# Attention and gated MLP in one fp32 kernel: both rows of a step turned and moved as one, values fetched whole a head ahead, two projections placed behind weighted sums

## What is computed

```python
k, q, v = (einsum('ihd,bpd->biph', W, xn) for W in (W_K, W_Q, W_V))
scores  = einsum('biph,biqh->biqp', k, q)
masked  = scores * mask - 1e10 * (1 - mask)
attn    = softmax(masked / sqrt(128))
z       = einsum('biqp,biph->biqh', attn, v)
out     = einsum('df,bqf->bqd', W_O, z_flat)
```

## Time and profile before

| | us |
|---|---|
| median of 3 runs | 1621.35 |
| lowest and highest | 1618.32, 1623.26 |
| the profiled execution's own time | 1623.7 |
| span of its profile | 1621.7 |
| PE busy | 1414.5 |
| POOL busy | 994.6 |
| DVE busy | 955.6 |
| ACT busy | 932.0 |

### The profile page before, as it was taken

How to read it: one execution, slowest core, us unless ns; L and a number is a source line. 1 busy time by engine, 2 the same in 40 slices (tenths; PEclk the granted TensorE clock), 3 DMA queues, 4 the chain that set the end, 5 groups by cost and what they waited for, 6 DMA issues and landing times.

```text
span 1621.7 us, 26479 instructions
## 1 busy us (share of the span) xinstructions
PE 1414.5 (87%) x8104; PEld 1254.5 (77%) x8104; DVE 955.6 (59%) x2133; ACT 932.0 (57%) x1879; POOL 994.6 (61%) x660
## 2 busy tenths in 40 slices
PE   4899999698879798989899888989898989898975
PEld 2788887487778787878888787878787878787875
DVE  7633201766657575767666666767675757575751
ACT  3222344466566666657575666666666666575753
POOL 3600000367667676767676777777767676767676
PEclk7999999899999999999999898999999999999988
DMA  3100266788788888989898989898989898979796
GB/s 131 62 1 0 61 191 170 209 243 236 214 227 244 229 241 231 239 232 239 233 243 229 242 228 242 230 240 223 251 218 247 219 250 223 245 225 245 217 243 175
DMA packets 236217, 335.13 MB, mean 207 GB/s; under 512 B 47120, under 2 KB 190608, under 8 KB 233616
## 3 DMA queue, kind: packets, MB, share of 16 engines
q1 hardware_dynamic: 236176, 334.65, 75.2%
HBM read 173.08 MB, written 161.48 MB: 206 GB/s over the span
## 4 chain that ended last, share of the span: by engine, by line
POOL 36%; issue 34%; PE 18%; DMA 5%; DVE 3%; SPq 2%; ACT 1%; POOLq 1%; DVEq 0%; ACTq 0%
POOL pt_lo L385 21%; POOL acc L376 8%; PE ps L832 6%; PE ps L833 6%; PE ps L834 6%; POOL v_lo L390 4%; DMA scratch<-raw 3%; SPq L284 2%; DMA v_lo<-all_values 1%; POOL wqk_hi L361 1%; DMA raw<-w3t 1%; POOL wo_lo L363 1%; DVE k_lo L677 1%; POOL wo_hi L361 0%; DVE w_raw L642 0%
## 5 line engine op out<-in xcount | busy, mean ns | idle before, releaser
L385 POOL TENSOR_TENSOR pt_lo<-pt_lo,pt_hi 128x640 fp32r<-128x640 f32 (+11 forms) x384 | 659.6, 1748 | 358.8 <-ACT pt_hi L558 358.3
L549 ACT ACTIVATE raw<-ps,had 128x1024 f32<-128x1024 f32 (+7 forms) x384 | 330.0, 867 | 256.0 <-DVE had L767 254.1
L832 PE MATMUL ps<-pt_hi,v_hi 128*128 128x256 f32 (+1 forms) x1152 | 340.5, 296 | 36.1 <-POOL v_lo L390 27.1
L774 DVE STREAM_TRANSPOSE raw<-raw 128x2048 f32<-128x2048 f32 (+15 forms) x256 | 322.0, 1292 | 78.9 <-ACT raw L549 76.4
L833 PE MATMUL ps<-pt_lo,v_hi 128*128 128x256 f32 (+1 forms) x1152 | 345.3, 300 | 0.0
L834 PE MATMUL ps<-pt_hi,v_lo 128*128 128x256 f32 (+1 forms) x1152 | 342.7, 297 | 0.0
L764 DVE TENSOR_REDUCE had<-ps 128x1 f32<-128x1024 f32 (+1 forms) x256 | 238.3, 951 | 84.0 <-PE ps L834 84.0
L558 ACT CAST pt_hi<-pt_lo 128x640 fp32r<-128x640 f32 (+11 forms) x384 | 282.2, 813 | 9.7 <-DMA pt_lo<-scratch 9.7
L832 PEld LDWEIGHTS ps<-pt_hi,v_hi 128*128 128x128 f32 x1152 | 238.9, 207 | 45.4 <-POOL v_lo L390 30.4
L832 PE MATMUL ps<-k_hi,q_hi 128*128 128x512 f32 (+3 forms) x640 | 238.9, 373 | 9.6 <-ACT raw L549 9.4
L833 PEld LDWEIGHTS ps<-pt_lo,v_hi 128*128 128x128 f32 x1152 | 237.7, 206 | 4.8
(11 more groups left out here) (102 smaller groups left out, 2382.1 us busy)
## 6 DMA issues: line engine op xcount, KB each, us to landing
all_values<-raw SPq DMA_DIRECT2D x16, 1024.0 KB, 5.1
scratch<-raw SPq DMA_DIRECT2D x16, 1024.0 KB, 6.1
pt_lo<-scratch SPq DMA_DIRECT2D x64, 256.0 KB, 4.6
v_lo<-all_values SPq DMA_DIRECT2D x64, 256.0 KB, 5.5
scratch<-raw SPq DMA_DIRECT2D x16, 960.0 KB, 6.3
pt_lo<-scratch SPq DMA_DIRECT2D x64, 240.0 KB, 4.4
scratch<-raw SPq DMA_DIRECT2D x16, 896.0 KB, 5.8
pt_lo<-scratch SPq DMA_DIRECT2D x64, 224.0 KB, 4.1
```

The source lines that it names most:

```text
L385: pool.tensor_tensor(lo, lo.bitcast(F32), hi.bitcast(F32), ALU.subtract).then_inc(pt_lo_done, 1)
L549: act.activation(to[:, first // P:(first + n) // P], ps[:, a * BANK:a * BANK + n].rearrange("p (i g k) -> p i g k", g=4, k=BLK), ACT.Exp, ...
L774: dve.transpose(v, v).then_inc(blocked, 1)
L832: pe.matmul(dst, a[0], b[0], start=start, stop=False, skip_group_check=True)
```

## The change

- **One move a step.** `raw` has 18 tiles a step. The small row's tiles start at an even place behind the big row's, so that the two rows of a step fill 17 tiles (even steps) or 18 with one between them (odd steps; POOL clears those columns once). DVE transposes all 18 tiles in one instruction after the third exponential; SP stores them in one DMA of 1152 KB to `scratch{s}` and loads them back in four DMAs, runs of 17 or 18 tiles. `p_to_hi` and `p_to_lo` are two pieces a step instead of three. `bring` of steps 4 and 6 waits for sums 1 and 3. Chunks lie in `pt_hi` and `pt_lo` with 18 tiles each pair; an odd row's lone key tile and the order of two halves in `z` follow from it.
- **Values.** One DMA of 1024 KB brings the next head's values to a new tensor `v_next` in SP's step 5, behind `send`; the splits read from there, in steps 1 (bank 3), 3 (bank 2) and 4 (banks 0 and 1).
- **Projections.** Q2 moves from step 0, ahead of the part of the big sum, to step 1, behind it; K3 from step 4, ahead of it, to step 3, behind it. Their splits move along on ACT and DVE. `split_qk` on POOL and the wait for it on PE are not edited.
- The program asks for a smaller scratch for descriptors (`dynamic_dma_scratch_size=1024`), which this kernel's DMAs, all issued by SP, do not use.

```diff
-    V_ITEMS = [3, 2, 1, 0]
+    V_ITEMS = [3, 2, 0, 1]
+    V_AT = {1: [3], 3: [2], 4: [0, 1]}
...
+        def first_tile(s, small):
+            return TILES - 2 * (s // 2) if small else 0
+        def tiles_of(s):
+            return 17 + s % 2
...
-            def send(h, s, small):
-                sp.wait_ge(blocked, 2 * (STEPS * h + s) + small + 1)
-                sp.dma_start(scratch[row_of(s, small)], raw_row(s, small)).then_inc(stored[small], 16)
+            def send(h, s):
+                sp.wait_ge(blocked, STEPS * h + s + 1)
+                sp.dma_start(scratch[s], raw_step(s)).then_inc(stored, 16)
...
-                    wait(sp, z_product, (z_count(h - 1, 5), z_count(h - 1, 7),
-                                         z_count(h, 1 if small else 0), z_count(h, 3 if small else 2))[m])
-                wait(sp, moved[small], 64 * (STEPS * h + s))
-                sp.wait_ge(stored[small], 16 * (STEPS * h + s + 1))
+                    wait(sp, z_product, (z_count(h - 1, 5), z_count(h - 1, 7), z_count(h, 1), z_count(h, 3))[m])
+                wait(sp, moved, 64 * (STEPS * h + s))
+                sp.wait_ge(stored, 16 * (STEPS * h + s + 1))
...
+            def bring_v(h):
+                wait(sp, v_lo_done, QUARTERS * h)
+                sp.dma_start(v_next[:, :], all_values[h].rearrange("p i d -> p (i d)")).then_inc(v_moved, 16)
...
                     hh, ss = step_before(h, s, 1)
                     if hh >= 0:
-                        bring(hh, ss, 0)
-                        bring(hh, ss, 1)
-                    if s == 1:
-                        bring_v(h, 3)
-                    send(h, s, 0)
-                    send(h, s, 1)
+                        bring(hh, ss)
+                    send(h, s)
+                    if s == 5 and h + 1 < HEADS:
+                        bring_v(h + 1)
...
             def p_to_lo(h, s, n):
-                j = row_of(s, n == 2)
-                a, b = ((0, 2), (2, 4), (0, 4))[n]
-                lo, hi = pt_row(pt_lo, j, a, b), pt_row(pt_hi, j, a, b)
+                lo, hi = (pt_step(t, s, 2 * n, 2 * n + 2) for t in (pt_lo, pt_hi))
...
             def transpose_blocks(h, s):
-                dve.wait_ge(exped, piece_count(h, s, 2 if small else 1))
-                v = raw_row(s, small).rearrange("p (b k) -> p b k", k=BLK)
+                dve.wait_ge(exped, exp_count(h, s, 2))
+                v = raw_step(s).rearrange("p (b k) -> p b k", k=BLK)
...
         def _(pe):
...
-                    if s == 0 and not over:
-                        project_kq(h, ("Q", 2))
                     if s == 2 and not over:
                         project_kq(h, ("Q", 1))
-                    if s == 4 and more and not over:
-                        project_kq(h, ("K", 3))
                     if s == 6 and more:
                         project_kq(h, ("Q", 0))
                     if not absent(Z_BIG[s][0]):
                         weighted_sum(h + Z_BIG[s][0], Z_BIG[s][1], s % 2)
+                    if s == 1 and not over:
+                        project_kq(h, ("Q", 2))
+                    if s == 3 and more and not over:
+                        project_kq(h, ("K", 3))
                     if s == 5 and more:
                         project_kq(h, ("Q", 3))
```

More of the change, by code:

```diff
@@ L159, in attention_ffn_kernel, with raw_step, pt_pair, pt_step @@
         all_values = nc.dram_tensor("all_values", [HEADS, P, TILES, P], F32).ap()
[L162 to L167, removed]
+        scratch = [nc.dram_tensor(f"scratch{s}", [P, RAW], F32).ap() for s in range(STEPS)]
+        def first_tile(s, small):
+            return TILES - 2 * (s // 2) if small else 0
+        def tiles_of(s):
+            return 17 + s % 2
+        def raw_step(s):
+            return raw[:, (s % 2) * RAW:(s % 2 + 1) * RAW]
+        def pt_pair(t, m):
+            return t[:, (m % 2) * PAIR:(m % 2 + 1) * PAIR].rearrange("p (b i q) -> p b i q", b=8, q=BLK)
         def pt_chunk(t, c):
             m = min(c, CHUNKS - 1 - c)
[L172 to L179, removed]
+            first = first_tile(2 * m, c == m)
+            return pt_pair(t, m)[:, :, first:first + 2 * c + 2, :]
+        def pt_step(t, s, first=0, last=4):
+            b = (s % 2) * 4
+            return pt_pair(t, s // 2)[:, b + first:b + last, 0:tiles_of(s), :]
         x_loaded = [sem(f"x_loaded{i}") for i in range(QUARTERS)]
@@ L411, in period @@
                         split_o(h, 2 * h + 3 if more else 2 * h + 2)
-                        v_to_lo(h, 1)
-                        v_to_lo(h, 0)
+                    for b in [] if over else V_AT.get(s, []):
+                        v_to_lo(h, b)
                     hh, ss = step_before(h, s, 2)
                     if not (first and s < 2) and not (over and s >= 2):
-                        for n in range(3):
+                        for n in range(2):
                             p_to_lo(hh, ss, n)
@@ L531, in v_to_hi @@
                 sl = slice(b * BANK, (b + 1) * BANK)
-                act.wait_ge(v_moved, 16 * v_count(h, b))
-                act.copy(v_hi[:, sl], v_lo[:, sl].bitcast(F32)).then_inc(v_hi_done, 1)
+                act.wait_ge(v_moved, 16 * h + 16)
+                if b == 3:
+                    wait(act, z_product, z_count(h - 1, 2))
+                elif b == 2:
+                    wait(act, v2_read, h)
+                elif b == 0:
+                    wait(act, z_product, z_count(h - 1, 7))
+                act.copy(v_hi[:, sl], v_next[:, sl]).then_inc(v_hi_done, 1)
             def exponential(h, s, e):
@@ L542, in exponential @@
                 if e == 0:
-                    for i in range(2):
-                        wait(act, stored[i], 16 * (STEPS * h + s - 1))
-                        if isinstance(h, int) and h == 0 and s < 2:
+                    wait(act, stored, 16 * (STEPS * h + s - 1))
+                    if isinstance(h, int) and h == 0 and s < 2:
+                        for i in range(2):
                             act.wait_ge(v_stored[i], 16 * TILES // 2)
-                to = raw_row(s, small).rearrange("p (g i k) -> p i g k", g=4, k=BLK)
-                act.activation(to[:, first // P:(first + n) // P],
+                to = raw_step(s).rearrange("p (g i k) -> p i g k", g=4, k=BLK)
+                at = first_tile(s, small) + first // P
+                act.activation(to[:, at:at + n // P],
                                ps[:, a * BANK:a * BANK + n].rearrange("p (i g k) -> p i g k", g=4, k=BLK), ACT.Exp,
@@ L554, in p_to_hi @@
             def p_to_hi(h, s, n):
[L555 to L558 removed]
+                act.wait_ge(moved, 64 * (STEPS * h + s + 1))
+                hi, lo = (pt_step(t, s, 2 * n, 2 * n + 2) for t in (pt_hi, pt_lo))
+                act.copy(hi, lo.bitcast(F32)).then_inc(pt_hi_done, 1)
             def z_to_hi(h, z):
@@ L996, in weighted_sum @@
                     i = tiles[n]
-                    lo = 4 if i == 2 * c + 1 else 0
+                    lo, hi = (0, 8) if i <= 2 * c else (4, 8) if z % 2 else (0, 4)
                     v = [t[:, i * P:(i + 1) * P] for t in (v_hi, v_lo)]
-                    p = [pt_chunk(t, c)[:, lo:8, i, :] for t in (pt_hi, pt_lo)]
-                    ins = mm3(bank(Z, lo * BLK, CHUNK_Q), v, p, n == 0, n == len(tiles) - 1)
+                    p = [pt_chunk(t, c)[:, lo:hi, i, :] for t in (pt_hi, pt_lo)]
+                    ins = mm3(bank(Z, lo * BLK, hi * BLK), v, p, n == 0, n == len(tiles) - 1)
                 if end == len(tiles):
```

105 lines of the change are left out of this document (39 added, 66 removed).

## The result

The changed kernel takes 1704.8 us (median of 4 runs, 1702.4 to 1709.4), the kernel before 1621.0 us beside it (1618.3 to 1623.3): a ratio of 1.0521, 95% interval 1.0494 to 1.0548. It is slower, as forecast, but by 84 us and not by 40, and 1704.8 lies above the range. The profiled execution has a span of 1700.6 us, against 1621.7.

A forecast was written before the change was run, and what follows sets the result against it. PE's and SP's loops were taken as nearly equal; K3's stall would delay step 2's load: 25.0 + 59.7 = 84.7 us a head against 81.8, 14 heads times 2.9 = 40 us, giving 1664 (1661 against the median), range 1590 to 1695.

The forecast's parts named there:

- S0: Issue of the load (bring) of step 0 on SP, from which K3's start and the load of step 2 were counted.
- The clock price: PE from K3 to sum 7: 6 us at half clock after the idle adds 3.0 us, 7.8 in all.
- the turn of 9.8 us: SP's queue, one merged store and load with start and receipt: 9.8 us a step, 9.5 to 10.1.
- start and receipt: Part of a turn on SP's queue beyond the bytes' transfer, with an empty queue: 1.7 us.
- The ends: Head 0, the end and one POOL memset: taken as 0, within 4 us.
- The lost overlap: The big row's load no longer starts when the big store alone is in: up to 1 us a turn.
- The transposes, counted 0: DVE's one transpose of 18 tiles, about 2.6 us, beside the DMAs: 0, upper end 0.6 us a step.
- PE's gaps decide: Rival: POOL's split early, so no K3 stall; SP's loop 79.3 us, in total 1586 us, or 1552; chance 0.15.
- the stall: PE's K3 in step 3 waits for POOL's split, 4 to 7 us a head, delaying sum 7 and step 2's load.
- No change: Rival: K3's stall at full clock and turns of 9.8 us, 81.7 us a head, 1620 us; chance 0.09.
- Faster by less: Rival: the stall stands but costs no clock, larger runs shorten the turn, 1578 to 1614 us; chance 0.14.
- Slower, but for the values: Rival: the values' 2.6 us count whole, step 5's load late for sum 4, 86.4 us a head, 1685; chance 0.08.

The follow-up runs named there:

- g1: The change with both projections back in their old places, leaving the values fetched whole and the merged move; 1647.2 us.
- f4: The kernel before with only the values fetched whole a head early, projections and turns as before; 1519.4 us.
- g2: g1 with the store of a step in two halves of the columns, each pair of loads waiting for its own half; 1571.6 us.
- m2: g2 with DVE's low part of K1 ahead of step 7's one transpose; 1532.8 us.
- f1: The change with POOL's split of Q and K one step earlier, in step 2 instead of step 3; 1650.4 us.
- f2: The change with K3 back in its old place in step 4, ahead of the big sum; 1648.0 us.
- n1: The whole change with POOL's split a step earlier, K1's low part ahead of the transpose, and the store in four quarters, each load waiting for its own; 1509.9 us.
- g3: g1 with SP issuing the store of step s ahead of the load of step s-1; 1734.3 us.

## Why the prediction was wrong, point by point

**What was right.** K3. Forecast were a wait of 4 to 7 us a head, some 14 of them: it is 6.2 on average, 15 times. K3 was to start at S0 + 17.2: it started at S0 + 16.9 (917.88 less 901.02). The load of step 2 was to be issued at S0 + 25.0: 24.1 on average. The clock price was too high: from K3 to that load I took 7.8 us, it was 6.6 (924.45 less 917.88), since the granted clock was 0.50 for some 3 us and 1.00 after that (0.76 over the 6 us shown), where 6 us of half clock were assumed:

```profile
917.90:919.00 1.10, 1.10 (x3) 0.91 (x4) 0.00 (x0) 0.00 (x0) 0.00 (x0) 0.50 1.00 423
...
920.00:921.00 1.00, 1.00 (x5) 0.81 (x5) 0.00 (x0) 0.16 (x1) 0.00 (x0) 0.58 0.14 55
921.00:922.00 1.00, 1.00 (x10) 1.00 (x10) 0.53 (x1) 1.00 (x3) 0.00 (x0) 1.00 0.00 0
```

Undoing the wait gives 54 to 57 us; the prediction has 75 (1661 less 1586).

**The step that failed: the turn of 9.8 us, 9.5 to 10.1.** Six turns and the values, from load 2 to the next head's load 0, were to be 59.7 us and are 62.4 (86.50 less 24.06). Turns that begin with a load of 17 tiles take 9.9 to 10.1, those of 18 tiles 10.3 to 10.4, and the values add 1.2 (11.6 at load 5; 0.9 was taken). One price stood for both kinds, and it was 0.2 us too low for the one and 0.5 to 0.6 for the other, at unchanged rates. By the prediction's own terms (5.0 or 5.3 for the load, 3.0 for the store, 1.7 for start and receipt) a turn is 9.7 or 10.0: rounding to 9.8 lost a little, and the term that was too small is the 1.7. What the measured turns leave beside 5.0 or 5.3 and 3.0 is 1.9 to 2.1. Together with K3's 0.9 us less, a head is 86.5 in place of 84.7, against a before that is 82.2 on average, not the 81.8 of the one head that was read: 4.3 us a head, not 2.9, 20 us in the run.

**The ends, "0, within 4 us", were 19.** The merge costs 7.5 us in a head of the loop (g1 82.8, f4 75.3), and it does not stop at the loop: g1 against f4 loses 6.7 us up to head 1's first load and 15.4 from head 15's. From the last load to the end it is 32.3 us in g1 for 27.5 in f4; that the last big row waits for the small one there is my reading, which no run tried. The two errors, 20 and 19 us, are the 39 us by which the profiled span missed.

**What hid in the sum.** The prediction compared whole loops (59.7 against 61.7) and so set off two large parts against each other without pricing them. The values were entered as a cost to SP of 0.9 us a head, with the gaps they make on PE as the gain; alone they give 6.9 us a head, because the old fetches made SP's turns longer too. The lost overlap of store and load was named, at "up to 1 us", and was in the 9.8; but no turn of the kernel before stood beside it, though the text reads one: from 838.80 to 847.4 a turn without values takes 8.6 us. So no rival asked what the change would be without the merge. It costs 7.5 us a head against f4, 0.9 us a turn on average, and with 128 turns and the ends 128 us. Cutting the store took 1.3 us off a turn but only 76 us off the run; another 39 us came when K1's low part was out of the way.

**The transposes, counted 0,** had a follower: K1's low part, 2.1 us a head of PE's time once the turn is short (39 us from g2 to m2). I had looked only at when the transpose ends, not at what DVE does behind it.

**The rivals.** "PE's gaps decide", without the stall 1552 to 1586, is refuted by f1 and f2: without it the change takes 1648 to 1650. "No change" took the stall at full clock and turns of 9.8; load 2 came at 24.1 in place of 22.0, and the turns were longer. "Faster by less" wanted shorter turns. "Slower, but for the values" has 86.4 us a head, next to the 86.5 measured, but by luck: the values add 1.2 us and not 2.6, and the rest is in the other turns. The gaps ahead of outputs did not go under 1 us (71 us in 53 waits).

**Rates and sizes.** The loads stayed at 226 GB/s with longer runs, as taken from the row of before. A turn got shorter with more and smaller DMAs, each load waiting for its part alone: 10.0 us with one store of 1152 KB, 8.7 with two, 8.1 with four. The Trainium skill's DMA: Bandwidth & Descriptors, Rules for kernel authors, wants many small transfers made into a large one, and names 64 KB as the size under which overhead is most of the time. Most transfers here were larger before the change already; where a load waits for the store, the runs show that one large transfer is the slower way. The Trainium skill's same page says, in its section Anatomy of one DMA, which is about DMAs issued by GpSimd, that the receipt of the last byte is most of a DMA's fixed cost. Whether that holds for the DMAs that SP issues no run here shows: the 1.9 to 2.1 us of a turn beyond its bytes are not split further.

## What to carry to other kernels

Two transfers with a dependent reader behind each are a pipeline; made one, the reader waits until all of it has landed, so price the lost overlap as so many us a turn times all turns before counting what is saved in issues and packets. Price each part of a change against the kernel before, alone: here +117 us, +56 us and -105 us hid in a net sum. A gap of an engine is worth filling only when its loop sets the pace: the same moved projections, with their split made early, gave 1.6 us with the queue as the bound and 44 us after the store had been cut.

## What the runs showed of the hardware

Fewer packets did not make less DMA work: the whole change took them from 236217 to 137138, and the DMA engines were busy 70.5 us a head in g1, merged, and in f4, with the rows apart. A store cut in four, with each load behind its own part, ran the turn in 8.1 us (n1), against 10.0 in one piece, with the same bytes. After an idle of 6.14 us PE got half its clock, 0.50, for some 3 us, in which it was busy without a break, and 1.00 after that; in the kernel before, behind an idle of 2.64 us, it was 0.50 over all of the 6 us read the earlier trace rows. And issuing the merged store ahead of a load that was ready cost 87 us (g3), since SP stood 876.5 us waiting for DVE's transposes with the load behind it.
